# A graph layer rebuilt: half of its source one-hots on ScalarE, identity and first weight split moved, transposed counts added by TensorE

## The reference

```python
def _L0_gnn_ref(x, edge_index, W, b, diffusion_weights):
    h = x @ W + b                               # 256x512 @ 512x512
    row, col = (edge_index[0], edge_index[1])   # 4352 edges
    adj = jnp.zeros((N, N)).at[row, col].set(1.0)
    adj = adj.at[col, row].set(1.0)
    adj = adj + jnp.eye(N)
    adj = adj / jnp.maximum(adj.sum(axis=1, keepdims=True), 1.0)
    out = diffusion_weights[0] * h
    cur = h
    for i in range(3):
        cur = adj @ cur
        out = out + diffusion_weights[i + 1] * cur
    return jax.nn.relu(out)
```

## Time and profile before

| | us |
|---|---|
| median of 3 runs | 480.96 |
| lowest, highest | 480.1, 481.13 |
| the profiled execution, its own time | 481.92 |
| its span in the trace | 480.1 |
| mean granted TensorE clock | 0.955 |
| TensorE busy | 443.1 (92%) |
| VectorE busy | 397.9 (83%) |
| ScalarE busy | 281.6 (59%) |
| GpSimd busy | 104.4 (22%) |

### The profile page before, as it was taken

The page is one execution under the profiler, slowest core; times in us unless marked ns, Lnnn a source line. Parts: engine busy times, 40 slices in busy tenths (PEclk is TensorE's granted clock), DMA queues, the critical chain, the costliest instruction groups (busy, mean ns, idle before and its releaser), DMA issues.

```text
span 480.1 us, 6137 instructions
## 1 busy us (share of the span) xinstructions
PE 443.1 (92%) x2208; PEld 354.5 (74%) x2208; DVE 397.9 (83%) x645; ACT 281.6 (59%) x306; POOL 104.4 (22%) x128
## 2 busy tenths in 40 slices
PE   3989899999999988899999998988999999999795
PEld 2655578888887868587899987656788888887674
DVE  8989768988989774777999888887798998979754
ACT  3245348787777753533444346345887888849541
POOL 5641000110010031157876200020001111000300
PEclk9999789999999997899999999979899999999797
DMA  7931545999998836788777244134789999967701
GB/s 251 305 130 44 186 173 211 348 335 360 358 367 311 339 148 253 286 303 296 203 201 248 72 156 155 41 137 175 284 297 348 342 404 363 364 226 289 281 2 45
DMA packets 25780, 115.67 MB, mean 241 GB/s; under 512 B 7036, under 2 KB 7708, under 8 KB 14864
## 3 DMA queue, kind: packets, MB, share of 16 engines
q1 hardware_dynamic: 18400, 93.90, 53.1%
q0 software_dynamic: 7056, 21.26, 13.4%
q10 hardware_dynamic: 288, 0.03, 0.1%
HBM read 108.63 MB, written 6.55 MB: 240 GB/s over the span
## 4 chain that ended last, share of the span: by engine, by line
PE 70%; DVE 14%; DMA 7%; ACT 4%; issue 3%; POOL 1%; DVEq 0%; ACTq 0%; SPq 0%; POOLq 0%
PE bank L1507 14%; PE bank L1508 14%; PE bank L1512 14%; PE bank L1883 3%; PE bank L1885 3%; PE bank L1500 3%; PE bank L1501 2%; PE bank L1502 2%; PE bank L1521 2%; PE bank L1772 2%; PE bank L1710 2%; DVE wlo L930 2%; DMA gath<-node_rows,src_i 2%; DMA raw<-in_weights_dram 2%; DMA y_tok<-y_rows,row_i 1%
## 5 line engine op out<-in xcount | busy, mean ns | idle before, releaser
L930 DVE TENSOR_TENSOR wlo<-raw,whi 128x2048 fp32r<-128x2048 f32 x73 | 165.3, 2287 | 19.5 <-ACT whi L675 18.7
L675 ACT ACTIVATE whi<-raw 128x2048 fp32r<-128x2048 f32 x73 | 137.6, 1914 | 11.0 <-PE bank L1852 6.4
L1507 PE MATMUL bank<-whi,xe_hi 128*128 128x512 f32 x192 | 79.1, 412 | 1.9 <-ACT xe_hi L704 1.4
L1508 PE MATMUL bank<-wlo,xe_hi 128*128 128x512 f32 x192 | 77.7, 405 | 0.0
L1512 PE MATMUL bank<-whi,xe_lo 128*128 128x512 f32 x192 | 52.6, 395 | 0.0
L1507 PE MATMUL bank<-whi,hT_hi 128*128 128x512 f32 (+1 forms) x124 | 50.2, 408 | 2.1 <-ACT hT_hi L732 2.1
L1508 PE MATMUL bank<-wlo,hT_hi 128*128 128x512 f32 (+1 forms) x124 | 48.4, 394 | 0.0
L617 POOL DMA_INDIRECT xg<-node_rows,idx x12 | 11.8, 985 | 160.8 <-DVE idx L1193 160.8
L650 POOL DMA_INDIRECT gath<-node_rows,src_i x34 | 42.0, 1234 | 14.9 <-DVE mp L1424 9.5
L1507 PEld LDWEIGHTS bank<-whi,xe_hi 128*128 128x128 f32 x192 | 37.1, 193 | 10.9 <-ACT xe_hi L704 1.9
L1508 PEld LDWEIGHTS bank<-wlo,xe_hi 128*128 128x128 f32 x192 | 37.2, 194 | 8.1
(11 more groups left out here) (307 smaller groups left out, 858.2 us busy)
## 6 DMA issues: line engine op xcount, KB each, us to landing
raw<-in_weights_dram SPq DMA_DIRECT2D x85, 1024.0 KB, 6.5
y_rows<-y_sb POOLq DMA_DIRECT2D x16, 256.0 KB, 6.0
ea<-in_ea_dram SPq DMA_DIRECT2D x8, 256.0 KB
node_rows<-xn POOLq DMA_DIRECT2D x4, 256.0 KB, 2.6
gath<-node_rows,src_i POOLq DMA_INDIRECT x34
x<-in_x_dram SPq DMA_DIRECT2D x1, 512.0 KB, 4.0
gw<-in_L_ffn_gw_dram SPq DMA_DIRECT2D x1, 512.0 KB, 10.6
node_rows<-A_sb POOLq DMA_DIRECT2D x2, 256.0 KB, 4.7
```

The lines of the kernel that those rows point to most:

```text
L675: act.activation(whi[n % SPL][:, :, :], raw[n % RAW][:, :, :], ACT.Copy).then_inc(hi_cut, 1)
L930: dve.tensor_tensor(wlo[n % SPL][:, :, :], raw[n % RAW][:, :, :], whi[n % SPL][:, :, :].bitcast(f32), ALU.subtract).then_inc(lo_cut, 1)
L1507: pe.matmul(ps, xh[:, blocks + k, :], whi[w % SPL][:, k, cs], start=first and k == 0, stop=False)
L1508: pe.matmul(ps, xh[:, blocks + k, :], wlo[w % SPL][:, k, cs], start=False, stop=False)
```

## The change

- The source one-hots of 16 tiles (`ACT_HOTS`: 5, 6, 8, 10, 15, 17, 18, 20, 22, 23, 25, 27, 28, 30, 32, 33) are made by ScalarE, in two activations each: Square of (column number minus source), then Relu of 1 minus that. The other 18, and all 34 destination ones, stay on VectorE.
- `dst_i` is loaded by SyncE's queue as its first DMA, ahead of x and W, instead of as the second of ScalarE's queue.
- VectorE writes `eye2` after the first five tiles instead of first. ScalarE clears `b_rows` and `gb_rows` (L832, a copy scaled by 0) instead of GpSimd. ScalarE also copies the identity into `g0_eye` once the first xn is there.
- ScalarE's bias split, and W's split right behind it, wait for all ten bias and batch-norm loads (they now share `bias_c`) instead of six.
- Chunk 1 (the next layer's first) is split by ScalarE after the first layer instead of within it.
- TensorE's counts are cut differently (`HOTS = (5, 7, 11, 28, ET)`): 11 tiles ahead of h instead of 19. After half n=0 of h come the other 23 tiles, then the first four mixed products of half n=1, the transposed counts, and the other four.
- The transposed counts and the counts are added in PSUM: two matmuls of the identity with the counts and four of the counts with the identity, instead of four transposes and an addition by VectorE.
- `g0_ra` is gone: ScalarE scales the adjacency while it takes the high part, VectorE while it subtracts. The bias addition and the split of h's second half move behind the reciprocal. u lies in banks 4 and 5 and the last product in banks 2 and 3. ScalarE splits the square ahead of v.

The diff, cut to its core:

```diff
-HOTS = (5, 7, 19, ET)
+HOTS = (5, 7, 11, 28, ET)
+ACT_HOTS = (5, 6, 8, 10) + tuple(t for t in range(14, ET) if t % 5 not in (1, 4))
+EARLY = 4
 # sync
+            sp.dma_start(dst_i[:, :], A["dst"]).then_inc(dst_in, 16)
             sp.dma_start(x[:, :, :], ...).then_inc(x_in, 16)
-                sp.dma_start(bn_c[:, i, :], ...).then_inc(bn_in, 16)
+                sp.dma_start(bn_c[:, i, :], ...).then_inc(bias_c, 16)
 # gpsimd
-            pool.memset(b_rows[:, :].bitcast(f32), 0.0).then_inc(gate["par"], 1)
-            pool.memset(gb_rows[:, :].bitcast(f32), 0.0).then_inc(gate["par"], 1)
+            pool.memset(ones[:, :], 1.0).then_inc(iota_ok, 1)
 # scalar
-            act.dma_start(dst_i[:, :], A["dst"]).then_inc(dst_in, 16)
-            act.wait_ge(bias_c, 16 * 6)
+            def src_hots(first, last):
+                for j in range(first, last + 1):
+                    if j < last:
+                        t = ACT_HOTS[j]
+                        if j >= 3:
+                            act.wait_ge(g0["hot_act"], j - 2)
+                        act.activation(g0_sq_dist[:, j % 3, :], iota_t[:, :], ACT.Square,
+                                       bias=g0_away[:, t:t + 1]).then_inc(g0["dist"], 1)
+                    if j > first:
+                        t = ACT_HOTS[j - 1]
+                        if t >= HOT0:
+                            act.wait_ge(g0["used"], t - HOT0 + 1)
+                        act.wait_ge(g0["dist"], j)
+                        act.activation(g0_S[:, t % HOT0, :], g0_sq_dist[:, (j - 1) % 3, :], ACT.Relu,
+                                       bias=ones[:, 0:1], scale=-1.0).then_inc(g0["hot_act"], 1)
+            for rows in (b_rows, gb_rows):
+                act.activation(rows..., iota_t... .to_broadcast([P, 3 * C // T, T]), ACT.Copy,
+                               scale=0.0).then_inc(g0["zeroed"], 1)
+            act.wait_ge(g0["hot"], 1)
+            src_hots(0, EARLY)
+            act.wait_ge(xn_ok, 1)
+            act.activation(g0_eye[:, :], ident, ACT.Copy).then_inc(g0["zeroed"], 1)
+            act.wait_ge(bias_c, 16 * 10)
             act.activation(b_hi[:, :], b_c[:, :], ACT.Copy).then_inc(gate["split"], 1)
             cut_to(1)
...
-            cut_to(2)
+            src_hots(EARLY, len(ACT_HOTS))
+            h_high(0)
             act.wait_ge(g0["used"], ET)
+            for counts in (g0_cnt_r, g0_cnt):
+                for n in range(NT):
+                    act.activation(counts[:, n, :], B[n][:, 0:T], ACT.Copy).then_inc(g0["cnt"], 1)
+            h_share(0, 0, 2)
+            for n in range(NT):
+                act.wait_ge(g0["adj"], n + 1)
+                act.activation(g0_ra_hi[:, n, :], g0_adj[:, n, :].bitcast(f32), ACT.Copy,
+                               scale=g0_rinv[:, n:n + 1]).then_inc(g0["ra_hi"], 1)
+            h_high(1)
+            h_share(0, 1, 2)
+            act.activation(g0_sq_hi[:, :, :], squared(), ACT.Copy).then_inc(g0["sq_hi"], 1)
 # vector
-            dve.wait_ge(iota_ok, 2)
-            for n in range(NT):
-                ins = dve.tensor_scalar(eye2[:, n, :], ...)
...
+                    if t not in ACT_HOTS:
+                        dve.tensor_scalar(g0_S[:, t % HOT0, :], iota_b[:, :], g0_src_f[:, t:t + 1], None,
+                                          ALU.is_equal)
...
+            edge_hots(HOTS[2], HOTS[3])
+            h_bias(0)
+            edge_hots(HOTS[3], HOTS[4])
+            h_low(0)
             dve.wait_ge(g0["turn_ps"], 1)
-            for n in range(NT):
-                ins = dve.tensor_tensor(g0_sum[:, n, :], B[6][:, n * T:(n + 1) * T], g0_cnt[:, n, :], ALU.add)
-            for n in range(NT):
-                dve.tensor_scalar(g0_ra[:, n, :], g0_adj[:, n, :].bitcast(f32), g0_rinv[:, n:n + 1], ...)
+            h_bias(1)
...
 # tensor
+                    if t in ACT_HOTS:
+                        pe.wait_ge(g0["hot_act"], ACT_HOTS.index(t) + 1)
...
+            h_rest(0, range(KB)).then_inc(g0["h_ps"], 1)
+            count_edges(HOTS[2], ET)
+            h_rest(1, range(KB // 2))
             pe.wait_ge(g0["cnt"], NT)
+            for a in range(NT):
+                pe.matmul(B[6][:, a * T:(a + 1) * T], g0_eye[:, :], g0_cnt_r[:, a, :], start=a == 0, ...)
             for a in range(NT):
                 for b in range(NT):
-                    ins = pe.transpose(B[6]..., g0_cnt[:, a, b * P:(b + 1) * P], ident)
+                    ins = pe.matmul(B[6]..., g0_cnt_r[:, a, b * P:(b + 1) * P], g0_eye[:, :], start=False, ...)
+            h_rest(1, range(KB // 2, KB)).then_inc(chunk_used, 1)
+            keep_busy(B[7], 2)
+            diffuse(0)
...
-            keep_busy(B[0], 6)
+            keep_busy(B[0], 2)
+            diffuse(1)
```

142 lines of the change are left out of this document (72 added, 70 removed).

## The result

The changed kernel takes **474.71 us** (median of 4 runs, 473.31 to 476.78), the kernel before 481.04 beside it (4 runs, 480.1 to 481.88). The ratio is 0.9858, 95% interval 0.9819 to 0.9897. The profiled execution took 473.31 us (span 471.4, mean granted clock 0.976).

The account below looks back on a forecast made before the run. The first layer was taken as a chain of waits: reciprocal 4.2 us ahead, 2.2 given back, last product 1.97 earlier, 1.8 after the clock's 0.15. From the median 480.96 that gave 479.2 us, range 477.4 to 481.4.

Parts of the forecast that it names:

- bias split: ScalarE, first layer: starts at 10.35 us instead of 9.39, waiting for the tenth bias load (beta).
- long loop: VectorE's long run of one-hots after `wlo` and both `g_xT_lo`: starts at 16.0 us instead of 19.33.
- counts' copies: After TensorE's counts: start at 23.8 us, the last one-hot at 23.4 plus 0.4 for its matmuls.
- reciprocal: First layer, 3.4 us after the counts: at 27.2 us, 4.2 ahead of before.
- last product: End of the first layer on TensorE: starts at 34.65 us instead of 36.62, 2.2 of the 4.2 given back.
- ScalarE's three splits: Chunk 1's split joins two others at the layer's end: done at 40.8 us, hidden by 2.2.
- ScalarE's pace: ScalarE's Square and Relu one-hots: 0.37 us per activation, 24 of them taking 8.9 us, done at 22.8.
- VectorE's loop: From 16.0 us: 26 one-hots (5.10), bias addition of half 0 (0.65), 8 one-hots (1.57), last written at 23.4.
- The loads, the slower side: Rival: a late tenth bias load holds W's split; 482.8 us for a landing at 14; chance 0.07.
- What lies behind is unchanged and starts when this ends.: Everything after the first layer's last product: simply starts 1.97 us earlier, 1.8 with the clock's 0.15.
- The clock: Rival: later clock falls, about 54 to 65 us, shift by 1.6 either way: 477.6 or 480.8; chance 0.09 each.
- P: Theory from the experiments, not the forecast: the first gather is held by a VectorE instruction that began just before it.

Follow-up runs that it names:

- after_best: Changed kernel with W's split ahead of the bias split, v ahead of the square, and 6 more fillers in the first gating: 472.55 us, ratio .9827.
- before_again: The kernel before, unchanged, timed and profiled again against itself: 480.99 us, ratio .9980.
- before_guard: Kernel before plus one unused VectorE reduction (256 x 3 elements) between `idx` and the subtraction, first layer of experts only: 479.21 us, ratio .9947.
- before_dstguard: Kernel before with `dst_i` first in SyncE's queue and the unused reduction that puts VectorE's subtraction behind the first gather: 479.34 us, ratio .9979.
- before_dst: Kernel before with `dst_i` loaded as SyncE's first DMA instead of ScalarE's second: 480.55 us, ratio .9983.
- before_clear: Kernel before with `b_rows` and `gb_rows` cleared by ScalarE instead of GpSimd: 480.94 us, ratio .9996.
- after_again: The changed kernel, unchanged, timed and profiled again beside the kernel before: 476.17 us, ratio .9899.
- before_fill: Kernel before with 6 more filler matmuls in TensorE's pauses of the first gating: 479.65 us, ratio .9967.
- after_dstback: Changed kernel with `dst_i` put back as ScalarE's second DMA: 478.01 us, ratio .9924.
- after_idx2: Changed kernel with one unused VectorE reduction (256 x 2 elements) ahead of the first gather's indices: 479.01 us, ratio .9963.
- best_guard: The fastest version (W's split first, v before the square, more fillers) plus the unused reduction ahead of VectorE's subtraction: 473.15 us, ratio .9828.
- after_delay: Changed kernel with 1280 useless VectorE columns before the low part of the square, and fillers raised from 8 to 14: 478.25 us, ratio .9945.
- after_idx: Changed kernel with three small unused VectorE instructions ahead of the one writing the first gather's indices: 476.62 us, ratio .9904.

## Why the prediction was wrong

Its working for the first layer held, step by step (forecast, then measured): bias split 10.35, 10.41, its idle time ended by the beta load; W split 10.66, 10.72; `wlo` 12.6, 12.65 after 0.21 idle; long loop from 16.0, 16.06; ScalarE's one-hots done 22.8, 23.17; h's first half split done 23.4, 23.68; VectorE's last one-hot 23.4, 23.9; counts' copies 23.8, 24.42; reciprocal 27.2, ended 27.95; last product 34.65, 35.27; ScalarE's three splits done 40.8, 40.60.

- **ScalarE's pace** was 0.40 and not 0.37 (498 ns alone, not 474). The prediction had named and set aside the figures of the Trainium skill, "ScalarE: Activation LUTs", section "What ACT_TABLE_LOAD costs", by which an activation takes an estimated 493 ns alone and the starts lie 0.40 apart; they were the right ones. It cost nothing: VectorE was later still.
- **VectorE's loop** was the mis-sized term: 0.5 us more than 5.10 + 0.65 + 1.57, between 18.0 and 21.8, where groups of three one-hots take 0.79 and 1.04 us as in the row at 19.64, and not 0.67 as at 23.23. The chain of waits stays on VectorE's two lines there; GpSimd issues small DMAs from 15.3 to 21.7, but it does so in after_best too, where the loop is stretched less; what stretched it was not tested. Of the 1.97 forecast for the layer 1.35 came. By these steps alone the forecast would have been less, not more.
- **The loads, the slower side:** beta landed 2.90 us after its issue. That rival did not happen.
- **The step that failed is "What lies behind is unchanged and starts when this ends."** Of the 6.3 us, 3.5 to 5 were made behind it: the layer shows 1.35 against the earlier trace rows and 2.8 against before_again. The instructions there were unchanged, but their order in time was not. Three things make up the difference, with the size that the runs give:
  1. *The held gather.* It was in 4 of 5 profiles of before's program without the guard, and not in the one that the prediction read. Taking it away gives 2.4 us in before_guard (ratio .9947, .9912 to .9982), and in before_dstguard 2.0 by the medians and 1.0 by the ratio, whose interval includes none. The new program reaches this place with `idx` 0.36 us earlier against ScalarE and VectorE's subtraction, by a shorter idle gap of VectorE ahead of it. No instruction of this place was changed, no term of the sum spoke of it, and why the gap is shorter stays open.
  2. *The clock.* The prediction had it as a rival of either sign, 1.6 us, chance 0.18. Its lucky side is what the pair of profiles shows (24.0 to 22.3 us from the last product to the first expert matmul). Over all profiles the fall there costs 1.1 to 1.7 us, with the change and without it. Over all executions 0.01 of mean granted clock goes with about 1.75 us within a kernel (from none to over 4 in single kernels); the kernel before had 0.968 on average (120 runs) and the changed one 0.973 (10 runs), which makes 0.8 us, an estimate. The span of the one profile after is lower still because its clock was 0.976.
  3. *A start that varies.* The first one-hot of the kernel before came at 5.20 in the profile that was read, and at 5.0 to 6.7 in six others; with `dst_i` first on SyncE's queue in the changed program at 3.3 to 3.5. The last product follows: 36.5 to 38.2 before, 35.3 to 35.6 after. So against before_again the layer gained 2.8 and not 1.35. But before_dst, which should take this away, gained nothing that can be measured.

The sum: 1.35 to 2.8 in the layer, 2.4 by the gather and 0.8 by the clock are 4.6 to 6.0, and the runs show 4.8 and 6.3. That they meet is no proof, since each median is good to about 0.8 us and before_dstguard gives the gather less. before_guard with 479.21 and before_dstguard with 479.34 leave 3 to 4.5 us to the changed kernel, of which its layer shows 1.2 to 2.6, the shorter gap ahead of `idx` 0.4 (takers at 14.8 and not 15.2), and the clock may be 0.8. Up to 1 or 2 us stay open. The direction was right by the layer's working; the other 3.5 us and more came from terms that the forecast did not have or put at nothing.

The held gather also fits a puzzle, without being shown by it: in the kernel before, time and granted clock hardly go together (correlation -0.39 over 120 runs; 0.03, -0.17 and -0.26 in before_again, before_dst and before_clear). By the profiles, an execution with the long fall pays for the clock but is spared the held gather (one profile of before's program), and one without it pays for the gather (four): two costs that exclude each other. With the gather free they go together: -0.84 and -0.85 in before_guard and before_dstguard, -0.80 in after_again. Not all kernels line up so: before_fill, whose profile has the held gather, shows -0.75, after_dstback -0.35; after_idx2, where P has the gather held in most executions, shows 0.10. Each is taken over 6 to 12 executions. And the forecast's profile looked harmless because it was the execution with the long fall.

The range failed for the same reason as the step. It was built from terms of one execution, and allowed for no event that this execution happened not to show. The clock's rival was right in kind, but its lucky end, 477.6, is nearly all that the range left room for.

## What to carry to other kernels

When a change moves the work ahead of a place by a fraction of a microsecond, look there for pairs that race: a GpSimd gather and a VectorE instruction with two SBUF inputs that become ready at nearly the same time. Here the order decided 2 us at the place itself. A useless VectorE instruction that keeps the order was a gain in before_guard and none in best_guard. Take the kernel before from more than one profile, because what the only one at hand doesn't show may be in most executions; and test "unchanged behind" by delaying the changed stage on purpose, as after_delay did, before crediting a gain to it.

## What the runs showed of the hardware

- The first gather of 128 rows takes GpSimd 1.06 us, and 3.10 to 3.12 when VectorE has begun a 128x2048 subtraction 0.10 to 0.12 us earlier; the later ones take 0.94 to 1.05, and 3.00 or 2.82 when it began 0.14 or 0.31 earlier. With listed starts within 0.05 us of each other both outcomes occur. The landing changes more than the instruction, 3.3 and 8.1 to 8.7 us.
- VectorE slows beside GpSimd's clears at the very start: before, the two writes of the identity take 1.57 us each; in before_clear, where only the clears are gone, they take 0.62 together, and after 0.61. From VectorE's groups of before (0 to 20 us), then the timeline of after:

```profile
L959 DVE TENSOR_SCALAR eye<-iota_t,node_id 128x256 f32<-128x256 f32 x2 | 3.1, 1566 | 1.3 <-POOL node_id L525 1.3
```

```profile
5.27 0.61 DVE L1018 TENSOR_SCALAR eye<-iota_t,node_id 128x256 f32<-128x256 f32 x2
```

- Square and Relu of 128x256 with a bias from a tile take 498 and 497 ns and start 0.40 apart:

```profile
L820 ACT ACTIVATE g_sq_dist<-iota_t,g_away 128x256 f32<-128x256 f32 x16 | 7.8, 498 | 0.0
L827 ACT ACTIVATE g_S<-g_sq_dist,ones 128x256 bf16<-128x256 f32 x16 | 7.8, 497 | 0.0
```

- Three small VectorE instructions behind a wait, 0.15 to 0.16 us each, delayed the next by 0.2 us in all (after_idx).
